# Weighted one-hots made on VectorE with two-scalar comparisons, tile by tile, and GpSimd taken out of the edge loop

## What is computed

```python
summed = jax.ops.segment_sum(x[src], dst, num_segments=n)             # layer 0: counts
deg = jax.ops.segment_sum(jnp.ones_like(src, dtype=x.dtype), dst, num_segments=n)
...
edge_weight = jax.nn.sigmoid(edge_attr @ conf_w.T + conf_b)[:, 0]     # layer 2: weights
out = jnp.zeros_like(x).at[col].add(x[row] * norm[:, None])
```

## Time and profile before

| | |
|---|---|
| three runs | 1886.28, 1888.68, 1889.43 us; median 1888.68 us |
| the profiled execution | 1888.74 us, its span (first to last instruction) 1887.1 us |
| VectorE busy over the whole span | 1272.5 us (67%) |
| GpSimd busy over the whole span | 694.7 us (37%) |
| the loop over groups, first comparison to last addition | 16.6 to 142.1 us of the span |
| granted TensorE clock in the loop | 1.00 |

### The profile page before, as it was taken

The page is one execution under the profiler, slowest core; times in us unless marked ns, Lnnn a source line. Parts: engine busy times, 40 slices in busy tenths (PEclk is TensorE's granted clock), DMA queues, the critical chain, the costliest instruction groups (busy, mean ns, idle before and its releaser), DMA issues. The chain is left out here.

```text
span 1887.1 us, 26506 instructions
## 1 busy us (share of the span) xinstructions
PE 1640.4 (87%) x8542; PEld 1270.9 (67%) x8542; DVE 1272.5 (67%) x1907; ACT 1029.8 (55%) x1286; POOL 694.7 (37%) x500
## 2 busy tenths in 40 slices
PE   4559699889988998899868599999999999999856
PEld 3555296678667867786744277777777777777543
DVE  8997646464655454544553279999989898998624
ACT  7633125232622352235211079999999999999611
POOL 3330100120012001200110388888888888887100
PEclk9999799989988998899989789999999999999978
DMA  2000421022002200120012476777777677778110
GB/s 92 0 0 6 139 69 35 1 74 73 23 6 69 77 19 28 46 95 1 29 63 103 138 166 136 149 146 148 140 148 145 143 143 147 146 141 194 22 50 28
DMA packets 112481, 159.34 MB, mean 84 GB/s; under 512 B 45066, under 2 KB 50570, under 8 KB 111794
## 3 DMA queue, kind: packets, MB, share of 16 engines
q0 software_dynamic: 77440, 89.44, 24.7%
q1 hardware_dynamic: 34962, 68.86, 11.0%
HBM read 145.73 MB, written 12.26 MB: 84 GB/s over the span
## 5 line engine op out<-in xcount | busy, mean ns | idle before, releaser
L1411 POOL DMA_INDIRECT edge_from_rows<-dst_table,edge_index x160 | 266.4, 1665 | 57.7 <-issue 45.2
L791 POOL TENSOR_TENSOR tr_r<-tr_r,tr_row_b 128x512 f32<-128x512 f32 x40 | 54.8, 1393 | 565.2 <-DVE C L1023 565.2
L194 PE MATMUL edge_z2p<-w_hi,edge_h_hi 128*128 128x512 f32 x640 | 261.6, 409 | 0.9 <-DVE edge_z L1568 0.8
L194 PE MATMUL edge_z2p<-w_hi,edge_h_lo 128*128 128x512 f32 x640 | 253.7, 396 | 0.0
L194 PE MATMUL edge_z2p<-w_lo,edge_h_hi 128*128 128x512 f32 x640 | 253.6, 396 | 0.0
L1401 POOL DMA_INDIRECT edge_from_rows<-src_table,edge_index x160 | 195.9, 1224 | 68.8 <-issue 34.9
L194 PEld LDWEIGHTS edge_z2p<-w_hi,edge_h_hi 128*128 128x128 f32 x640 | 120.6, 188 | 56.3 <-issue 30.6
L194 PEld LDWEIGHTS edge_z2p<-w_hi,edge_h_lo 128*128 128x128 f32 x640 | 120.6, 188 | 29.2
L194 PEld LDWEIGHTS edge_z2p<-w_lo,edge_h_hi 128*128 128x128 f32 x640 | 120.7, 189 | 25.2
L959 ACT ACTIVATE tr_probs<-tr_scores,tr_nmax 128x640 f32<-128x640 f32 x80 | 66.2, 828 | 110.1 <-DVE tr_nmax L1080 107.2
L194 PE MATMUL front_sum_ps<-front_to_onehot,front_from_onehot 128*128 128x192 f16 x800 | 74.3, 250 | 59.5 <-DVE front_sums L556 46.3
(11 more groups left out here) (268 smaller groups left out, 4128.4 us busy)
## 6 DMA issues: line engine op xcount, KB each, us to landing
edge_attr<-in_attr_T SPq DMA_DIRECT2D x80, 128.0 KB
tr_w_raw<-in_m SPq DMA_DIRECT2D x8, 1024.0 KB, 5.3
tr_w_raw<-in_wv SPq DMA_DIRECT2D x5, 1024.0 KB, 5.3
tr_w_raw<-in_wq SPq DMA_DIRECT2D x5, 1024.0 KB, 5.3
agg<-edge_sum_rows POOLq DMA_DIRECT2D x40, 128.0 KB
tr_w_raw<-in_wk SPq DMA_DIRECT2D x4, 1024.0 KB, 7.0
tr_w_raw<-in_wo SPq DMA_DIRECT2D x4, 1024.0 KB, 5.3
tr_cw_raw<-in_cond_w SPq DMA_DIRECT2D x5, 768.0 KB, 5.6
```

What stands on the lines that cost most here:

```text
L194: mm = pe.matmul(out, a, b, start=(n == 0), stop=(n == last))
L791: pool.tensor_tensor(r[:, i, :], r[:, i, :], row_b[:, :], ALU.add).then_inc(bias_added, 1)
L1411: pool.indirect_dma_start(out=from_rows[ring][:, j, :], out_offset=None, in_=k.dst_table, in_offset=bass.IndirectOffsetOnAxis(ap=index[rin ...
```

## The change

GpSimd's loop is removed, and with it the semaphore `weighted`; TensorE waits for `to_ready` instead. VectorE still writes part 0 with one comparison, and then writes parts 1 and 2 itself, tile by tile: a `tensor_scalar` that compares the 64 columns of the window with the tile's destination (a pointer scalar, one value for each partition, from `dst_f`) and multiplies by the tile's weight (a second pointer scalar, from `wf[0]` or `wf[1]`). The weights' halves are now kept in fp32 in two buffers; `wb` keeps the high half in fp16 for the rounding alone. `to_ready` is raised by the last of the eight new instructions.

```diff
-                n = sweeps(pool)
-                with pool.Fori(0, n * (GROUPS // RING) + GROUPS // RING) as t:
-                    for a in range(RING):
-
-                        pool.wait_ge(to_ready, t * RING + (a + 1))
-                        settle(k, pool)
-                        shape = [P, TPG, 2, WIN]
-                        weights = wb[:, bass.ds((t * RING + a) % GROUPS * TPG, TPG), :]
-                        pool.tensor_tensor(to_onehot[a][:, :, 1:3, :], to_onehot[a][:, :, 0:1, :].to_broadcast(shape),
-                                           weights[:, :, :, None].to_broadcast(shape), ALU.mult).then_inc(weighted, 1)
...
-                        pe.wait_ge(weighted, u + 1)
+                        pe.wait_ge(to_ready, u + 1)
...
-                step(dve.tensor_copy(wb[:, :, 0], wr[:, :]))
-                step(dve.tensor_copy(wf[:, :], wb[:, :, 0]))
-                step(dve.tensor_tensor(wr[:, :], wr[:, :], wf[:, :], ALU.subtract))
-                step(dve.tensor_scalar(wb[:, :, 1], wr[:, :], SCALE_LO, None, ALU.mult))
+                step(dve.tensor_copy(wb[:, :], wr[:, :]))
+                step(dve.tensor_copy(wf[0][:, :], wb[:, :]))
+                step(dve.tensor_tensor(wr[:, :], wr[:, :], wf[0][:, :], ALU.subtract))
+                step(dve.tensor_scalar(wf[1][:, :], wr[:, :], SCALE_LO, None, ALU.mult))
...
-                    dve.tensor_tensor(to_onehot[a][:, :, 0, :], iota16[:, bass.ds(start, WIN)][:, None, :].to_broadcast(shape),
-                                      dst16[:, bass.ds(tile0, TPG)][:, :, None].to_broadcast(shape),
-                                      ALU.is_equal).then_inc(to_ready, 1)
+                    window = iota16[:, bass.ds(start, WIN)]
+                    dve.tensor_tensor(to_onehot[a][:, :, 0, :], window[:, None, :].to_broadcast(shape),
+                                      dst16[:, bass.ds(tile0, TPG)][:, :, None].to_broadcast(shape), ALU.is_equal)
+                    for j in range(TPG):
+                        tile = bass.ds(tile0 + j, 1)
+                        for part in range(2):
+                            ins = dve.tensor_scalar(to_onehot[a][:, j, 1 + part, :], window, k.dst_f[:, tile],
+                                                    wf[part][:, tile], ALU.is_equal, ALU.mult)
+                    ins.then_inc(to_ready, 1)
```

More of the change, by code:

```diff
@@ L219, in front @@
         wz, wr = sb("wz", [P, TILES]), sb("wr", [P, TILES])
-        wb = sb("wb", [P, TILES, 2], F16)
-        wf = sb("wf", [P, TILES])
+        wb = sb("wb", [P, TILES], F16)
+        wf = [sb("wf_high", [P, TILES]), sb("wf_low", [P, TILES])]
         from_onehot = [sb(f"from_onehot{a}", [P, TPG, NP], F16) for a in range(RING)]
@@ L250, in front @@
         away_ready, last_ready = sem("away_ready"), sem("last_ready")
-        from_ready, to_ready, weighted, group_ready, added = (
-            sem(n) for n in ("from_ready", "to_ready", "weighted", "group_ready", "added"))
+        from_ready, to_ready, group_ready, added = (
+            sem(n) for n in ("from_ready", "to_ready", "group_ready", "added"))
         h_ready, maxed, logs_ready = sem("h_ready"), sem("maxed"), sem("logs_ready")
```

## The result

The changed kernel takes 1926.84 us (median of four runs, 1923.65 to 1927.80); the kernel before took 1889.06 us beside it. The ratio is 1.020, with a 95% interval of 1.0182 to 1.0217: slower by 38 us. The profiled execution took 1927.36 us with a span of 1925.6 us, 38.5 us more than before.

What follows compares the result with a forecast made beforehand. VectorE, busy 125.42 of 125.50 us in the loop, was taken to bound it. 1888.7 us plus 70.6 for 336 small comparisons less 31.2 of stall gave 1928 us, range 1914 to 1947 (forecast band 1918 to 1936).

Steps and rivals of the forecast that it cites:

- The stall: In the loop, GpSimd's instruction holds up VectorE's third 640-column comparison, 0.78 us a group; its removal gives −31.2 us.
- The step of a small comparison: Start-to-start time of each new 64-column, two-pointer comparison in the loop: 0.21 us; 336 of them add 70.6 us.
- The sum: 70.6 us added less 31.2 us removed: the loop ends at 181.5 us, all behind it moves by +39.4 us.
- The sequencer: VectorE's register work for the eight new instructions, about 1.05 us a group in the loop, stays hidden beside their 1.68 us.
- rival (b): In the loop the sequencer sets the pace, pointers partly hidden: 0.13 to 0.18 us a step, 1901 to 1918 us; 11%.
- TensorE's clock: It may fall in the loop, costing nothing inside; behind the loop nothing is added and 2 us allowed.
- The signs: Expected in the new profile's loop: 640-column comparisons never above 0.39 us, small ones 0.27 to 0.30 us long.
- the upper bound: Highest step for a small comparison in the loop, its whole duration with no overlap: 0.286 us, 96 us in all.
- rival (d): No overlap in the loop: sequencer loads uncovered or each short instruction waits for its forerunner: 0.286 us each, 1954 us; 8%.
- (a): Pointers are free in the loop's short instructions: 0.08 us a step, 26.9 us in all, 1884 us, faster; 4%.
- (c): Short comparisons in the loop run unpacked: 0.26 us a step, 1945 us, or 1936 if only at odd starts; 15%.
- (e): The loop's stall doesn't come from GpSimd, so nothing is taken away and +70.6 us give 1959 us; 1%.

## Why the prediction was right

The forecast was 1928 us, measured 1926.84; the terms, by the prediction's steps:

- *The stall*: −31.2 us forecast from the earlier trace rows. In the changed kernel 3.94 − 8 × 0.207 leave 2.28 us a group, so all of it is gone. Removed alone it gave −30.0 us, and that this is so near to 31.2 is in part luck: 5.0 us of new idle time in the loop stand against 3.4 us gained behind it. Its cause (packed comparisons held by GpSimd) is shown by the run that puts GpSimd back and by the two that move it.
- *The step of a small comparison*: 0.21 us taken, between 0.20 and 0.22; measured 0.207. The parts were right one by one: 0.06 us for each pointer, and 0.085 us for base and columns, where I had 0.080.
- *The sum*: 336 × 0.207 = 69.6 us, less 31.2, is +38.4; the loop grew by 38.2 us and the span by 38.5. The loop's end was forecast at 181.5 and is 180.2; most of that is the step, which I had rounded up.
- *The sequencer*: hidden, as said, at 3.94 us a group. The step of 0.085 us without register work shows that the 0.13 us of rival (b) was a pace of issue and not of VectorE.
- *TensorE's clock*: it did fall in the loop, to a mean of 0.87 with drops to 1.2 GHz, and nothing came of it there: at 1.2 GHz the 20 matmuls of a group take 3.36 us in place of 1.81 (those that start at 42.30), which still fits into 3.94, and they wait for the addition in any case. At the loop's exit the mean is 0.57 over 180.4 to 187.0 us against 0.75 before, and the stretch up to the transformer's stage took 76.6 us against 75.6, so 1 us.
- *The signs*: two of those named were set too tight, without weight for the time. The 640-column comparisons take up to 0.41 us, not 0.39 at most, and the small ones up to 0.33, not 0.30.
- *The working*: the terms of the upper bound add up to 0.288 us, not 0.286 (0.7 us in the sum); the thirteen and five instructions of rival (d) count the addition itself.

Of the rivals, (a) (free pointers) falls with the runs that take pointers away one by one: they are not free. The formula of the Trainium skill (VectorE: DVE Perf Modes, The TRN2 errata — SBUF-src ops pay a fixed extra latency per instruction) gives an estimated 77 ns, and the comparison without pointers measures 85; what it lacks here is 0.06 us for each pointer. (c) (unpacked) falls by the step, 0.207 and not 0.26, and by the held comparison. All 336 steps lie between 205 and 210 ns. The windows' starts, worked out from the inputs as the lowest destination of each group, are odd in 19 groups and even in 21, and the mean steps are 207.5 and 206.6 ns, so the alignment of which (c) speaks makes no difference here. (d) and (e) fall by the same rows. What I didn't foresee is that the stall's removal alone would run into the sequencer at 2.29 us; it cost the forecast nothing, since at 3.94 us a group the sequencer has the time. Nor did I foresee that the stretch behind the loop would move by 3.4 us in the two fastest kernels.

## What to carry to other kernels

When two engines are in each other's way, first look at which instruction of the one meets the other, and whether a later release puts it beside an instruction that doesn't care: here moving one semaphore gained 26 us, while moving the work lost 38. When work goes from one wide instruction to several narrow ones, count instructions and pointer operands before columns: at 64 columns, an estimated 0.19 of 0.207 us had nothing to do with the data (64 columns at 0.25 ns are 0.016). And read steps from start to start: durations overlap, and 336 × 0.30 us less the stall would have put this change at +70 us in place of +38.

## What the runs showed of the hardware

GpSimd's own instruction takes 1.19 us where it starts in the middle of a 640-column comparison and 1.04 us where it starts behind one, and also 1.04 us beside the 64-column comparisons. The 0.15 us fit a comparison that holds GpSimd until it is through, but no run tests that by itself.

The durations of VectorE's small comparisons crept from 0.29 to 0.33 us in the loop while their steps stayed at 0.207 us. I have no cause for it; it costs nothing.

The stretch between the loop and the transformer's stage has the same matmuls in every kernel, and TensorE is busy for over nine tenths of it. It took 72.1 to 72.2 us without weights and with the release by the second comparison, 73.5 to 73.8 with one pointer, with GpSimd put back and with the release by the third, and 75.5 to 76.6 in the other five. A loop in which TensorE idles less doesn't order them: the one of 193 us, with GpSimd put back, is among the middle three. At the ends the granted clock of the stretch was 0.99 and 0.94. What decides it stays open.

The transformer's stage, which no kernel here touches, took 744.7 us before, 739.0 in the profile with one pointer and 757.0 in the one without. The windows of that stage, in this order for the kernels with one pointer and without, are these:

```profile
233.40:972.40 739.00, 656.44 (x3272) 533.48 (x3272) 396.09 (x731) 264.74 (x459) 78.10 (x50) 0.93 0.15 48
```

```profile
215.10:972.10 757.00, 664.46 (x3272) 540.57 (x3272) 396.19 (x731) 264.70 (x459) 78.78 (x50) 0.91 0.15 47
```

VectorE, ScalarE and GpSimd did the same work in the same time; TensorE's mean clock was 0.91 in place of 0.93. The profile with one pointer is its kernel's fastest execution, 1895.20 us against a median of 1907.19, so the difference is at least in part one between executions and not between kernels. That stage alone moves a single run by up to 18 us here, as much as many a change. I haven't tested what sets it off. A term of a few microseconds is better read from the loop's own window than from the whole time.
